# GpSimd takes gate products and projection sums, exponentials span two banks, warm transpositions stand at both ends, and the plan is drawn anew

## What is computed

```python
def step(h, fis):              # layer 1: gated recurrence over the tokens
    f_t, i_t, s_t = fis
    h = f_t * h + i_t * s_t
    return (h, h)
...
y = o * h
z = x + y                      # then LayerNorm with gamma, beta
...
out = r * einsum(k_act, W_v)   # layers 2 and 4: r = sigmoid(xr W_r), k_act = relu(xk W_k)^2
...
scores = einsum(qc, k) * scale # layer 3: causal attention, 16 heads of 16 channels,
p = softmax(scores - m)        # 4096 keys, m the maximum of a row; then projection Wo, bias bo
```

## Time and profile before

| | |
|---|---|
| median of 3 runs | 1793.16 us (1791.85 to 1793.26) |
| the profiled execution | 1792.9 us, its span 1791.2 us |
| TensorE busy | 1726.6 us, 96% |
| VectorE busy | 1553.3 us, 87% |
| ScalarE busy | 1310.6 us, 73% |
| GpSimd busy | 544.3 us, 30% |
| mean granted TensorE clock | 0.993 of full speed |

### The profile page before, as it was taken

The page is one execution under the profiler, slowest core; times in us unless marked ns, Lnnn a source line. Parts: engine busy times, 40 slices in busy tenths (PEclk is TensorE's granted clock), DMA queues, the critical chain, the costliest instruction groups (busy, mean ns, idle before and its releaser), DMA issues.

```text
span 1791.2 us, 34351 instructions
## 1 busy us (share of the span) xinstructions
PE 1726.6 (96%) x12684; PEld 751.4 (42%) x12684; DVE 1553.3 (87%) x3102; ACT 1310.6 (73%) x2759; POOL 544.3 (30%) x841
## 2 busy tenths in 40 slices
PE   6799999999999999999999999999999999999997
PEld 5675555454444543344333453333433323333224
DVE  5778888889989999999998999999999999999702
ACT  2236576677687578866888758888788888888994
POOL 4336447534323722325221341321222101110001
PEclk9899999999999999999999999999999999999999
DMA  3132012002100310011000020000200000000000
GB/s 109 42 79 60 24 36 45 21 21 45 35 7 8 63 29 6 8 35 35 6 12 13 7 51 2 12 23 2 46 6 13 17 6 2 13 1 8 1 1 12
DMA packets 56955, 42.99 MB, mean 24 GB/s; under 512 B 8788, under 2 KB 56788, under 8 KB 56788
## 3 DMA queue, kind: packets, MB, share of 16 engines
q1 hardware_dynamic: 54548, 39.75, 9.2%
q10 hardware_dynamic: 2240, 1.05, 0.4%
HBM read 24.00 MB, written 16.25 MB: 22 GB/s over the span
## 4 chain that ended last, share of the span: by engine, by line
PE 34%; DVE 14%; ACT 5%; issue 1%; POOL 0%; DVEq 0%; POOLq 0%; ACTq 0%
DVE span_max L1308 13%; PE psum L1557 11%; PE psum L1536 7%; PE psum L1504 6%; PE psum L1371 4%; ACT probs L1078 4%; PE psum L1365 3%; PE psum L1359 1%; PE psum L1566 0%; PE psum L1511 0%; PE psum L1519 0%; DVE rows L1249 0%; DVE small L1167 0%; DVE rows L1301 0%; ACT oT L1085 0%
## 5 line engine op out<-in xcount | busy, mean ns | idle before, releaser
L1308 DVE TENSOR_REDUCE span_max<-psum 128x1 f32<-128x512 f32 (+3 forms) x2304 | 1312.8, 637 | 73.0 <-PE psum L1504 53.8
L1078 ACT ACTIVATE probs<-psum 128x512 f32<-128x512 f32 (+3 forms) x2304 | 1116.8, 573 | 203.0 <-PE psum L1536 200.0
L1557 PE MATMUL psum<-probs,v_aug 128*17 128x512 f32 (+3 forms) x4608 | 565.4, 562 | 2.8 <-POOL probs L967 2.0
L1504 PE MATMUL psum<-k_stack,q_stack 48*128 48x512 f16 (+3 forms) x2304 | 515.6, 362 | 7.3 <-DVE span_max L1308 5.1
L1536 PE MATMUL psum<-q_stack,k_stack 50*128 50x512 f16 (+3 forms) x2304 | 512.9, 365 | 4.4 <-ACT probs L1078 1.6
L1536 PEld LDWEIGHTS psum<-q_stack,k_stack 50*128 50x128 f16 x2304 | 138.9, 93 | 508.9 <-ACT probs L1078 439.5
L967 POOL TENSOR_SCALAR_AFFINE_SELECT probs<-probs 128x512 f32<-128x512 f32 x128 | 81.1, 636 | 566.6 <-ACT probs L1078 566.4
L1504 PEld LDWEIGHTS psum<-k_stack,q_stack 48*128 48x128 f16 x2304 | 166.8, 94 | 177.7 <-DVE span_max L1308 97.2
L1557 PEld LDWEIGHTS psum<-probs,v_aug 128*17 128x17 f32 x4608 | 76.5, 95 | 130.6 <-issue 112.5
L1004 ACT ACTIVATE rows<-psum,cols 128x256 f32<-128x256 f32 x128 | 53.7, 471 | 88.8 <-PE psum L1365 88.3
L1511 PE MATMUL psum<-mask_keys,mask_rows 64*128 64x64 bf16 x1024 | 91.5, 189 | 0.0
(11 more groups left out here) (122 smaller groups left out, 1412.2 us busy)
## 6 DMA issues: line engine op xcount, KB each, us to landing
q_stack<-q_parts SPq DMA_DIRECT2D x192, 32.0 KB, 2.0
k_stack<-k_parts SPq DMA_DIRECT2D x42, 128.0 KB, 4.6
rows<-in_x SPq DMA_DIRECT2D x16, 256.0 KB, 2.7
q_parts<-rows SPq DMA_DIRECT2D x32, 128.0 KB, 1.9
k_parts<-rows SPq DMA_DIRECT2D x32, 128.0 KB, 2.0
out<-rows SPq DMA_DIRECT2D x16, 256.0 KB, 2.2
x_rows<-rows SPq DMA_DIRECT2D x14, 256.0 KB, 2.2
rows<-x_rows SPq DMA_DIRECT2D x14, 256.0 KB, 2.7
```

The source lines that it names most:

```text
L1078: act.activation(probs[:, tile % PROBS, i, q0:], bank(b)[:, q0:], ACT.Exp, scale=SCALE / QK_SCALE).then_inc(exp_done, 1)
L1308: nc.vector.tensor_reduce(span_max[:, s % SPAN_RING, row:row + 1, k0 // SPAN:k0 // SPAN + 1], bank(b)[:, 0:k1 - k0], AX.X, ALU.max).then_i ...
L1504: ins = nc.tensor.matmul(bank(b)[:, 0:k1 - k0], q_stack[row:row + SCORE_ROWS, s % Q_RING, u, qt * P:(qt + 1) * P], k_stack[row:row + SCORE ...
L1557: ins = nc.tensor.matmul(pv_bank[32 * h:32 * h + VW, q0:], v_aug[:, j, g * HG + h, :], probs[:, tile % PROBS, h, q0:], start=(j == 0), sto ...
```

## The change

**Gates and sums on GpSimd.** For units from `EARLY` (4) on, `is`, `y` and `z` leave VectorE: GpSimd adds 1 to i and to o (`i.affine`, `o.affine`), multiplies (`p.is`, `p.y`), and adds the transposed result to the stream (`p.z`) after ScalarE has copied it from PSUM (`z.copy`, into the buffer of o). For units below 14, `x3` becomes a copy by ScalarE (`x3.copy`) and a sum on GpSimd (`p.x3`). The bank is then free after the copy, but the o gate of the next unit waits for `p.z`, and the next attention transposition's copy for `p.x3`, since they share a buffer.

**Exponentials over two banks.** In steps 28 to 31 the planner places the two halves of a pair of heads in neighbouring banks where it can, and one `exp2` reads both, if both are ready within 100 ns.

**Warm transpositions.** Where the plan sees TensorE idle for over 1000 ns before the first or after the last product with v, it puts in transpositions of the identity into bank 7, to 0.75 of the gap.

**Plan.** `MOST`, `AHEAD` and `WORTH` have new values; `LEAD` too, which allows every unit at any time both before and now.

```diff
-MOST = {"max": 4, "scores": 4, "job": 4}
+MOST = {"max": 4, "scores": 5, "job": 5}
...
+def gates_late(u):
+    return u >= EARLY
...
-AHEAD = 18603
-LEAD = 13.5
-SOON, TWO = 0, -2100
+AHEAD = 36199
+LEAD = 18.25
+NEAR = 0
+SOON, TWO = 0, -3100
-WORTH = {"max": 2400, "dve": 1.0, "scores": 2650, "act": 1.562, "half": -2100, "pv": 2100, "stay": -6850,
-         "two": 1750, "ring": -5400, "last": -6600, "job": 1350, "age": 0.005, "same": 750, "after": -5250,
-         "rest": 750}
+WORTH = {"max": 3000, "dve": 1.6, "scores": 2950, "act": 1.953, "half": -2700, "pv": 1200, "stay": -11650,
+         "two": -5450, "ring": -8700, "last": -10200, "job": -900, "age": 0.001, "same": 2700, "after": -4350,
+         "rest": 1050}
...
+        gap = at - max(free["PE"], *half_free)
+        if e == "PE" and gap > 1000 and (not summed or summed == len(TILES)):
+            order.append(("warm", int(WARM_SHARE * (gap - 400) / WARM)))
...
+                other = [o for o in ready["ACT"] if o[0] == "exp" and o[1] == k[1] and o[2] == k[2] ^ 1]
+                if (other and other[0][3] - k[3] == other[0][2] - k[2] and TILES[k[1]][0] >= EXPS_SINCE and
+                        ready["ACT"][other[0]] <= at + TOGETHER):
...
+                elif op[0] == "p.z":
...
+                    pool.wait_ge(z_copied, u - EARLY + 1)
+                    nc.gpsimd.tensor_tensor(stream, stream, a_y, ALU.add).then_inc(z_ready, 1)
...
+                elif op[0] == "i.affine":
+                    u = op[1]
+                    pool.wait_ge(gate_ready["i"], u + 1)
+                    nc.gpsimd.tensor_scalar(a_i, a_i, 1.0, 1.0, ALU.mult, ALU.add).then_inc(i_affine, 1)
+                elif op[0] == "p.is":
+                    u = op[1]
+                    pool.wait_ge(i_affine, u - EARLY + 1)
+                    pool.wait_ge(gate_ready["s"], u + 1)
+                    nc.gpsimd.tensor_tensor(a_i, a_i, a_s, ALU.mult).then_inc(is_ready, 1)
...
+                elif op[0] == "p.y":
+                    u = op[1]
+                    pool.wait_ge(h_ready, u + 1)
+                    pool.wait_ge(o_affine, u - EARLY + 1)
+                    nc.gpsimd.tensor_copy(h_last, a_f[:, :, UNIT - 1:UNIT])
+                    nc.gpsimd.tensor_tensor(a_o, a_o, a_f, ALU.mult).then_inc(y_ready, 1)
...
+                elif op[0] == "p.x3":
+                    u = op[1]
+                    pool.wait_ge(bo_added, u + 1)
+                    pool.wait_ge(x3_copied, u + 1)
+                    nc.gpsimd.tensor_tensor(c_stream, c_stream, c_proj, ALU.add).then_inc(x3_ready, 1)
...
+                        elif gates_late(u - 1):
+                            act.wait_ge(z_ready, u)
...
+                elif op[0] == "z.copy":
+                    u = op[1]
+                    act.wait_ge(full["yT"], u + 1)
+                    act.activation(a_y, bank_tok(BANK["yT", u]), ACT.Copy, scale=0.25).then_inc(z_copied, 1)
...
+                elif op[0] == "exp2":
...
+                    for half in range(2):
+                        act.wait_ge(scored[half], PAIRS * tile + i // 2 + 1)
+                    if tile >= PROBS and exps % HG == 0:
+                        act.wait_ge(pv_done, tile - PROBS + 1)
+                    act.activation(probs[:, tile % PROBS, i:i + 2, q0:],
+                                   psum[:, b * CHUNK:(b + 2) * CHUNK].rearrange("p (h q) -> p h q", h=2)[:, :, q0:],
+                                   ACT.Exp, scale=SCALE / QK_SCALE).then_inc(exp_done, 2)
...
+                if name == "warm":
+
+                    if scores:
+                        pe.wait_ge(o_copied, len(STEPS))
+                    else:
+                        pe.wait_ge(pv_cleared, 1)
+                    for n in range(op[1]):
+                        nc.tensor.transpose(pv_bank[:, 0:P], ident[:], ident[:])
```

More of the change, by code:

```diff
@@ L327, in width, with apart, bank_for @@
         return CHUNK - max(0, j - STEPS[s][1] * TT) * P
-    def bank_for(kind, t):
+    def apart(b, kind, half, t):
+        if half is None or kind == "scores" and TILES[scored][0] < EXPS_SINCE or kind == "max":
+            return False
+        if beside[kind] is not None:
+            return b != beside[kind]
+        other = b + (1, -1)[half]
+        return not 0 <= other < BANKS or bank_free[other] > t + NEAR
+    def bank_for(kind, t, half=None):
         taken = [b for b in range(BANKS) if bank_free[b] == never]
@@ L335, in bank_for @@
             return never, None
-        b = min(idle, key=lambda b: (max(bank_free[b], t), holder[b] != kind, b))
+        b = min(idle, key=lambda b: (max(bank_free[b], t), apart(b, kind, half, t), holder[b] != kind, b))
         at = bank_free[b]
@@ L391, in on_pe @@
             base = max(t, half_free[h]) if division == "half" else whole + SWITCH
-            can["scores"] = (max(base, bank_for("scores", t)[0], seen["place", TILES[scored][0]]), h)
+            can["scores"] = (max(base, bank_for("scores", t, h)[0], seen["place", TILES[scored][0]]), h)
         at = ready_pv(summed)
```

105 lines of the change are left out of this document (80 added, 25 removed).

## The result

The changed kernel takes **1785.4 us**, median of 5 runs (1783.9 to 1786.8), against 1793.2 us of the kernel before in the same batch (5 runs, 1791.9 to 1793.5). The ratio is 0.9958, with a 95% interval of 0.9948 to 0.9969. It is faster by 7.8 us, where 22 were forecast; the time lies inside the stated range of 1748 to 1797 us. The execution profiled took 1785.7 us, its span 1783.9.

The account below looks back on a forecast made before the run. It took two nearly full engines, TensorE and VectorE, coupled by seven PSUM banks, as the middle's limit. Terms 10 + 6 + 4 + 2 = 22 us off 1792.9 gave 1771 us, range 1748 to 1797.

Parts of the forecast that it names:

- 10 (middle): Middle stretches, moved work and new plan: 10 us gain, taken between estimates of 7 and 12.
- 6 (doubles and tail): Tail after the last reduction: 4 us from 69 joined exponentials, 2 from four exponentials fewer.
- 4 and 2 (warm): Warm transpositions in TensorE's gaps: 4 us gained at the start, 2 at the end.
- If both count alike: Middle: VectorE's 33 us less and TensorE's 8 more each count half, a gain of 12 us.
- 37 us: VectorE's busy time taken away by moving is, y, z twelve times and x3 fourteen times.
- As a sum it costs nothing: GpSimd's 81 us of new work costs nothing in total, with 79 us free in steps 4 to 9.
- Transpositions leave the clock: Rival, both ends: slow rows stay, 6 us of gain gone and 1 paid, 1778 us; chance 0.16.
- TensorE sole limit: Rival: TensorE alone paces the middle, which costs 9 us while the ends give 12, 1790 us; chance 0.14.
- VectorE sole limit: Rival: TensorE's 9% are all slack, the middle gives 35 us in place of 10, 1746 us; chance 0.13.
- Gate chain: Rival: gates through GpSimd take 3.6 us more a unit, 43 us if all twelve are exposed, 1814 us; chance 0.14.
- the three signs of being wrong: Reductions waiting on TensorE more than before, scans waiting on GpSimd, or products waiting on masks.
- my rule: Middle: each stretch lasts the larger engine's demand plus its present gap; the larger ones sum 1444 to 1437, gain 7 us.

Follow-up runs that it names:

- the old work under refitted numbers: Kernel before plus warm transpositions alone, with the planner's numbers fitted again and no moved work: 1783.7 us, 0.9949 of the kernel before.
- the filler on VectorE: Changed kernel with 50 reductions of 512 SBUF columns put on VectorE where work was moved off it: 1801.9 us, 1.0052 of the kernel before.

## Why the prediction came out as it did

**The sign held, but not for the reason that carried it.** The sum was 10 (middle) + 6 (doubles and tail) + 4 + 2 (warm). Measured, it is about -5.6 for the middle, 1 for the doubles with some 1.6 beside it in the tail, and 8.5 for the warm blocks. These add up to 5.5, against the 7.3 us by which the two profiled spans differ; each is known to a us or two. The gain measured is about the warm part's alone, and the forecast's sign is right although its largest term has the wrong one.

**The step that failed** is "I take 10, between these two, since both engines are over 90% full nearly everywhere", on the new plan and the moved work. The middle grew from 1530.8 to 1536.4 us, so the term is -5.6 and not 10. Three things in that step were wrong:

1. *The worth of VectorE's time.* "If both count alike" put each us at a half. Taken off with the order held, 25.2 us gave 5.6 (0.22 each); put on, 26.6 cost 16.5 (0.62 each). TensorE's gave 0.34 (up to 0.47 with the clock). I read the difference between removing and adding as that of a fixed order, in which added time pushes what follows and removed time leaves gaps that nothing fills; the runs show the two prices, not their reason, and they come from two different orders, the kernel before and the changed one.
2. *The amount.* "37 us" left VectorE; its busy time fell by 20. About 12 us came back through instructions that got longer (the scans 22.6 to 27.2, and so on in the lines shown), and 5 more through the reductions (1312.8 to 1317.5). Not all of the 12 is the moved work's doing: with it shortened, VectorE's busy time fell by 5.0 us only. What stands beside GpSimd's older work changes with the order too: in the old work under refitted numbers the scan takes 841 ns and the line of L1451 284, with nothing moved.
3. *GpSimd's part at nothing.* "As a sum it costs nothing" was right, as GpSimd kept 70 us free in steps 4 to 9. Yet its new work costs 7.7 us, by waits and by stretching.

The measured prices come within 3 us of the account of the middle. With GpSimd's part shortened, VectorE is 24.9 us below the kernel before and TensorE has 8 more: 24.9 x 0.22 - 8 x 0.34 = 3 us of gain. The middle of that run is 1531.0 us, no shorter than the 1530.8 before. So even with GpSimd's part taken away the moved work and its plan gave nothing there, and GpSimd's part, 5.4 us of it in the middle, makes the loss measured.

**The warm transpositions** were the term best supported and still too small, 6 forecast and 8.5 (or 7.3, added alone) measured. I halved the slow stretches twice, once for the speed and once for what lies on the chain. At the start most of the 10.5 us at most lay on the chain: 6.0 us by the timelines, 7.3 by the close of step 3 when they were added alone, 8.2 when they were taken out. From the last unit's attention output to the end of the span it was 30.4 us before (1760.82 to 1791.2) and is 28.9 now (1754.98 to 1783.9), 1.5 gained, close to the 2 of the forecast.

**The exponentials** were mis-sized: 69 doubles x 0.015 us is 1 us in place of 4. The slope of means over widths is not the time between starts in a full row of them. The tail is 4.1 us shorter by the table (4.3 by the maxima): 1.5 by the clock, 1 by the doubles, and the rest, 1.6, fits the four exponentials fewer behind the last reduction, for which I had 2; no run has that part alone.

**The rivals.** *Transpositions leave the clock*: falls, by both runs with and without them. *TensorE sole limit*, 1790: its number is the nearest to the result, and for the middle it said "costs 9" where 5.6 were measured; but the filler on VectorE cost 16.5 us, which it says should cost none. *VectorE sole limit*: falls by 0.22 per us. *Gate chain*: real, and on the path, but at 7.7 us with the stretching in it, far from 43. It never decided the sign.

**Of what was to be seen**: VectorE 1533 (1516 forecast), GpSimd 615 (625), step 9 at 378.3 (360), step 15 at 614.2 (605), step 23 at 1076.9 (1071), step 31 at 1686.5 (1675), a tile of the tail 1.93 us (1.83), doubles of 0.97 us (1.0), the clock 0.98 and 1.00 at the ends (above 0.95 and 0.97). Two of the three signs of being wrong are there: the reductions' idle time before them, most of it waits for TensorE, rose from 73.0 to 84.0 us, and scans wait 3.9 us for GpSimd, though for its older scaling of f (L989), where it was 0.5. Stretch by stretch, my rule (the larger engine's demand plus the old gap) gives 220, 240, 465 and 600 us, and measured are 228, 236, 463 and 610. The 360 for step 9 did not even follow from it, which would have said 374. The rule misses most in steps 24 to 31, by 10 us: it took VectorE's 580 as the larger and so counted TensorE's 14 more (549 to 563) as nothing, where by the measured price they are 5. And in steps 4 to 9 it misses by 8, where GpSimd is busiest and its work costs most. Three slips of the prediction are small and change no conclusion: its four stretches give VectorE 31 us less and not 33, so the bound with VectorE alone is 33 in place of 35; a tile with two instructions less of 0.054 us is 1.85 us and not 1.83; and the range starts at 1748 where the case that it names is at 1746.

**What stays open**: how the 7.7 us divide into waits for GpSimd and stretched VectorE instructions, why VectorE's 25 us less in the changed order gain nothing even without them, why time taken off and time put on have different prices, and which waits make a plan 23 to 38 us longer when its numbers do not fit the work.

## What to carry to other kernels

Ask of each part of a mixed change what it gives alone: here a dozen lines that fill idle time, and pay mostly at the start, gave the whole gain, and 80 us of moved work gave none. Where two engines are both over 90% full in an order written for fixed durations, a us taken off one of them was worth a fifth to a half, and one added about half or more; measure that price once with a shortened or a filler instruction before moving work for it. And when work moves, choose the plan anew for it before judging it, since the numbers of a plan are worth more (23 to 38 us) than the move.

## What the runs showed of the hardware

**Transpositions of fp32 raise and hold TensorE's clock.** After 59 of them the first projection ran at 0.86 us a half, the level of 2.4 GHz; without them it is 1.70, the level of 1.2 GHz, and after the two pauses shown, of 4.76 and 2.46 us, projections ran at that level again. Within the first block the transpositions themselves went from 0.21 to 0.11 us apart. The granted clock of the start went from 0.95 to 1.00 when nothing else was changed. The Trainium skill ("TensorE: Matmul & The Clock Gate", Part 4) says that the fast clock does not engage for transpose mode; for these transpositions, fp32 of 128x128 against the identity, the trace does not agree. No record says whether they ran in that mode, so this bounds the sentence and need not contradict it.

**VectorE's instructions that read SBUF twice take longer beside GpSimd's.** Scans took 734 ns alone and 1024 beside a GpSimd instruction, in one and the same execution. With 71 us more of GpSimd's work the scan's mean went from 796 to 947 ns, L1399's from 522 to 577, while the reductions from PSUM stayed within 2 ns of 637; with that work shortened the two came to 881 and 518. The Trainium skill ("SBUF — State Buffer", Who interferes with whom) gives the rule, two SBUF inputs against a GpSimd instruction that reads SBUF, and the trace agrees. The prediction named this rule, and took it for the scans alone. One instruction that reads a single SBUF operand, L1446 of 128x16, also took longer beside GpSimd (292 ns against 173), while L1290, which reads one of 128x256, did not (414 both ways).

**An exponential over two banks** takes 0.965 us for 1024 columns, back to back, against 0.98 for two of 512: in a full row, joining two saves some 0.015 us.
